# One signal and one read per head for the maxima scores of an attention kernel

## The reference

```python
q = (layer_norm(x) @ q_w); k, v = ctx @ k_w, ctx @ v_w          # 16 heads of 16
s = jnp.einsum('bnhd,bmhd->bhnm', q, k) * scale
s = jnp.where(mask, -big, s)                                    # stages 0, 2, 3
x = x + (jax.nn.softmax(s) @ v) @ proj_w + proj_b
x = x + gelu(layer_norm(x) @ fc1_w + fc1_b) @ fc2_w + fc2_b     # stages 0, 2, 4
```

## Time and profile before

| what | value |
|---|---|
| median of 3 runs | 5233.54 us |
| the profiled execution, by its own time | 5238.51 us |
| its span, first to last instruction | 5236.7 us |
| mean granted TensorE clock | 0.959 of full speed |
| TensorE matmuls busy | 4648.7 us (89%) |
| VectorE busy | 3017.8 us (58%) |
| ScalarE busy | 2310.5 us (44%) |
| stages 0 to 4, about | the first 3960 us |

### The profile page before, as it was taken

The page is one execution under the profiler, slowest core; times in us unless marked ns, Lnnn a source line. Parts: engine busy times, 40 slices in busy tenths (PEclk is TensorE's granted clock), DMA queues, the critical chain, the costliest instruction groups (busy, mean ns, idle before and its releaser), DMA issues.

```text
span 5236.7 us, 70053 instructions
## 1 busy us (share of the span) xinstructions
PE 4648.7 (89%) x24484; PEld 1877.5 (36%) x24484; DVE 3017.8 (58%) x6690; ACT 2310.5 (44%) x3011; POOL 963.7 (18%) x831
## 2 busy tenths in 40 slices
PE   5898898888887989999888888888877999999999
PEld 2333333333332333343444433333333333333333
DVE  5766676556667767666455665445422545554554
ACT  3444454456664444434444444443432433333332
POOL 0111111101110111111111111110111433333333
PEclk9999999999999999999999999999988999999999
DMA  1111111121111100001111211110111000000000
GB/s 55 35 42 56 38 48 42 35 73 65 56 65 48 37 35 31 30 29 51 62 59 57 68 56 45 39 35 33 43 36 52 1 13 13 13 13 13 1 13 9
DMA packets 152323, 201.92 MB, mean 39 GB/s; under 512 B 18993, under 2 KB 102321, under 8 KB 150706
## 3 DMA queue, kind: packets, MB, share of 16 engines
q1 hardware_dynamic: 151986, 197.31, 11.2%
HBM read 128.86 MB, written 68.42 MB: 38 GB/s over the span
## 4 chain that ended last, share of the span: by engine, by line
PE 64%; DVE 14%; issue 12%; ACT 4%; DMA 4%; POOL 1%; SPq 1%; DVEq 0%; ACTq 0%; POOLq 0%
PE psO L707 7%; PE small L635 7%; PE psT L764 6%; PE small L642 6%; PE psS L663 6%; PE psT L682 5%; PE psT L908 4%; DVE out L1141 3%; PE psT L773 3%; PE small L773 3%; DVE nmb L1144 3%; PE psT L635 2%; PE psT L873 2%; PE psO L923 2%; PE psT L642 2%
## 5 line engine op out<-in xcount | busy, mean ns | idle before, releaser
L966 ACT ACTIVATE probs<-psT 128x1024 f32<-128x1024 f32 (+3 forms) x1280 | 1160.9, 961 | 1054.1 <-PE psT L682 858.4
L1144 DVE TENSOR_REDUCE nmb<-psS 128x2 bf16<-128x1024 f32 x512 | 627.8, 1226 | 332.7 <-PE psS L663 331.9
L682 PE MATMUL psT<-low 32*128 32x512 f32 (+3 forms) x5120 | 771.7, 621 | 49.7 <-ACT probs L966 28.2
L1141 DVE CUSTOM_DVE_ANT_0 out<-psS,pens_sb 128x512 f32<-128x512 f32 x1024 | 665.4, 687 | 81.4 <-issue 60.0
L663 PE MATMUL psS<-out 32*128 32x512 bf16 (+3 forms) x2560 | 494.1, 383 | 219.1 <-DVE nmb L1141 121.4
L707 PE MATMUL psO<-probs,V 128*32 128x512 f32 (+3 forms) x5120 | 673.6, 600 | 1.2 <-ACT probs L966 1.0
L1343 DVE TENSOR_REDUCE parts<-psS 128x2 bf16<-128x1024 f32 x256 | 314.9, 1230 | 522.0 <-PE psS L895 522.0
L1081 ACT ACTIVATE probs<-psT 128x1024 f32<-128x1024 f32 x256 | 262.2, 1024 | 526.0 <-PE psT L911 526.0
L663 PEld LDWEIGHTS psS<-out 32*128 32x128 bf16 x2560 | 121.1, 91 | 900.7 <-DVE nmb L1141 367.5
L764 PE MATMUL psT<-out,W 128*128 128x512 f32 x768 | 378.8, 618 | 0.5
L1460 POOL TENSOR_TENSOR oN<-oN,probs 128x1024 f32<-128x1024 f32 x128 | 300.7, 2349 | 316.1 <-ACT probs L1081 315.8
(11 more groups left out here) (163 smaller groups left out, 5822.6 us busy)
## 6 DMA issues: line engine op xcount, KB each, us to landing
o_mid<-out SPq DMA_DIRECT2D x160, 256.0 KB, 2.0
oN<-o_mid SPq DMA_DIRECT2D x160, 128.0 KB
oN<-r_mid SPq DMA_DIRECT2D x80, 256.0 KB
x_mid<-xe SPq DMA_DIRECT2D x40, 512.0 KB, 3.0
xw<-x_mid SPq DMA_DIRECT2D x36, 512.0 KB, 4.0
xe<-x_mid SPq DMA_DIRECT2D x36, 512.0 KB, 4.8
cT<-ctxT SPq DMA_DIRECT2D x20, 512.0 KB, 7.3
W<-wm SPq DMA_DIRECT2D x6, 1024.0 KB, 8.0
```

What stands on the lines that cost most here:

```text
L682: last = nc.tensor.matmul(psT[j][:, q0:S], Kf[rows_of(j), q, a, c, kt * P:(kt + 1) * P], Qf[rows_of(j), q, a, c, q0:S], start=True, stop=p ...
L966: nc.scalar.activation(probs[:, i % 2, two, q0:S], psT_all[:, two, q0:S], ACT.Exp, scale=float(DH) ** -0.5)\
L1141: nc.vector.tensor_tensor_reduce(junk[:, e, 0:n], psS[e][:, 0:n], penalty, 1.0, -3.0e38, ALU.add, ALU.max, nmb4[:, g, qt, at:at + 1]).then ...
L1144: nc.vector.tensor_reduce(nmb4[:, g, qt, row:row + 33:32], psS_both[:, :, 0:n], AX, ALU.max)\
```

## The change

Each head of a pair gets a semaphore of its own in both directions: s_full0 and s_full1, s_read0 and s_read1. TensorE waits for head e's bank in front of head e's matmul, and each matmul signals. VectorE waits for head e's scores in front of head e's read, and each read signals. In stages 1 and 4 the one reduction over 1024 columns becomes two over 512. In stages 0, 2 and 3 each of the two reads gets its own memset and its own wait for the head's read one pair earlier. Fill "m" waits for both semaphores. The function `reads`, which told the two forms' counts apart, goes.

```diff
@@ -254,11 +254,6 @@
 N_WO = C * D + 2 * D
 
 
-def reads(s):
-
-    return 2 if s in (*MASKED, CAUSAL) else 1
-
-
 def per_unit(s):
 
     mlp = 1 if s in MLP else 0
@@ -269,7 +264,7 @@
         "stats": norms, "moments": norms, "variance": norms, "rstd": norms, "normed": norms,
         "stats_m": mlp, "moments_m": mlp, "variance_m": mlp, "rstd_m": mlp, "normed_m": mlp,
         "biased": 1 + mlp, "q_low": C,
-        "s_full": 2 * STEPS, "s_read": 2 * STEPS * reads(s),
+        "s_full0": 2 * STEPS, "s_full1": 2 * STEPS, "s_read0": 2 * STEPS, "s_read1": 2 * STEPS,
         "f_full": FC * mlp, "f_read": FC * mlp, "z_full": mlp, "z_read": mlp,
         "st_full": 2 * STEPS, "exp_done": 2 * STEPS,
         "pv_done": STEPS, "o_out": G, "o_stored0": 32, "o_stored1": 32,
@@ -656,13 +651,12 @@
                         pe.wait_ge(small_read, place.start() + 1)
                     pe.wait_ge(sem["q_low"], count("q_low", u, c + 1))
 
-                if positive(r := count("s_read", u, (2 * i + k) * reads(u.s))):
-                    pe.wait_ge(sem["s_read"], r)
                 for e in range(2):
                     j = 2 * (1 - k) + e
-                    last = nc.tensor.matmul(psS[e][:, 0:n], Qb[rows_of(j), q, a, c, qt * P:(qt + 1) * P], Kb[rows_of(j), q, c, 0:n],
-                                            start=True, stop=True)
-                last.then_inc(sem["s_full"], 1)
+                    if positive(r := count(f"s_read{e}", u, 2 * i + k)):
+                        pe.wait_ge(sem[f"s_read{e}"], r)
+                    nc.tensor.matmul(psS[e][:, 0:n], Qb[rows_of(j), q, a, c, qt * P:(qt + 1) * P], Kb[rows_of(j), q, c, 0:n],
+                                     start=True, stop=True).then_inc(sem[f"s_full{e}"], 1)
 
             def exp_scores(place, u, i):
 
@@ -723,7 +717,8 @@
                 if kind == "k" and use == place.first(who, "k0") and u.s not in OWN_KEYS and u.s:
                     pe.wait_ge(sem["ctx_in"], count("ctx_in", u, 16))
                 if kind == "m":
-                    pe.wait_ge(sem["s_read"], count("s_read", u, 2 * T * (int(use[1]) + 1) * reads(u.s)))
+                    for e in range(2):
+                        pe.wait_ge(sem[f"s_read{e}"], count(f"s_read{e}", u, 2 * T * (int(use[1]) + 1)))
                 if kind == "q" and use == place.first(who, "q0"):
                     pe.wait_ge(qkv_in, 16 * (u.s + 1))
                 if kind == "y" and use == place.first(who, "y"):
@@ -1127,22 +1122,21 @@
                 g, qt = divmod(i, T)
                 n = (qt + 1) * P if u.s == CAUSAL else S
                 row = MAX_ROW[g % 2] + DL * (1 - k)
-                dve.wait_ge(sem["s_full"], count("s_full", u, 2 * i + k + 1))
-                if reads(u.s) == 2:
-                    penalty = tri_row[:, S - n:S] if u.s == CAUSAL else masking(pensM, u)[:, qt * S:(qt + 1) * S]
-                    if u.s == 0 and i == 0 and k == 0:
-                        dve.wait_ge(sem["pens"], count("pens", u, 1))
-
-                    if positive(r := count("s_read", u, 2 * (2 * i + k))):
-                        dve.wait_ge(sem["s_read"], r)
-                    nc.vector.memset(scratch[:, 6:7], 0.0)
-                    for e in range(2):
-                        at = row + 32 * e
+                if u.s == 0 and i == 0 and k == 0:
+                    dve.wait_ge(sem["pens"], count("pens", u, 1))
+                for e in range(2):
+                    at = nmb4[:, g, qt, row + 32 * e:row + 32 * e + 1]
+                    dve.wait_ge(sem[f"s_full{e}"], count(f"s_full{e}", u, 2 * i + k + 1))
+                    if u.s in (*MASKED, CAUSAL):
+                        penalty = tri_row[:, S - n:S] if u.s == CAUSAL else masking(pensM, u)[:, qt * S:(qt + 1) * S]
+
+                        if positive(r := count(f"s_read{e}", u, 2 * i + k)):
+                            dve.wait_ge(sem[f"s_read{e}"], r)
+                        nc.vector.memset(scratch[:, 6 + e:7 + e], 0.0)
                         nc.vector.tensor_tensor_reduce(junk[:, e, 0:n], psS[e][:, 0:n], penalty, 1.0, -3.0e38,
-                                                       ALU.add, ALU.max, nmb4[:, g, qt, at:at + 1]).then_inc(sem["s_read"], 1)
-                else:
-                    nc.vector.tensor_reduce(nmb4[:, g, qt, row:row + 33:32], psS_both[:, :, 0:n], AX, ALU.max)\
-                        .then_inc(sem["s_read"], 1)
+                                                       ALU.add, ALU.max, at).then_inc(sem[f"s_read{e}"], 1)
+                    else:
+                        nc.vector.tensor_reduce(at, psS[e][:, 0:n], AX, ALU.max).then_inc(sem[f"s_read{e}"], 1)
 
             def limit(u, i):
 
```

## The result

The changed kernel takes 5188.3 us (median of 4 runs, 5179.8 to 5195.9) where the kernel before takes 5234.3 beside it: a ratio of 0.991, 95% interval 0.9897 to 0.9923, or 46 us less. The forecast was 5222 and its range began at 5200: the sign was right, the size was not. The profiled execution has a span of 5177.0 us against 5236.7.

What follows compares the result with a forecast made beforehand. TensorE's instruction stream was taken as the bound, with 194 us of idle time before maxima scores all the change could reach. Terms -28 + 7.4 + 3.7 + 5 = -12 us gave 5222 us, range 5200 to 5252.

Steps and rivals of the forecast that it cites:

- first wait: Maxima pair held up for VectorE's read when the pair before was not itself held up; 229 of 324 waited pairs.
- (2): Stages 1 and 4: one reduction becoming two costs 0.07 us at each of 106 first waits, 7.4 us on.
- (3): Stages 0, 2 and 3: one memset more costs 0.03 us at each of 123 first waits, 3.7 us on.
- (4): VectorE already late, with layer-norm work at a unit's start: added work delays what follows, about 5 us on.
- (1): Head 0's matmul starts once its bank is read: no gain at a first wait, 28 us off at 54 second waits.
- second wait: Maxima pair held up for VectorE's read directly behind another held-up pair; 95 of 324 waited pairs.
- (5): Extra waits on TensorE and VectorE and their register operations in loops: costed at nothing, hidden by instructions queued ahead.
- (6): MLP block: TensorE's array has no gap there, so its 16 pairs per unit neither gain nor lose.
- A: Rival, slower: VectorE's second instruction is not overlapped and pays its fixed part at first waits; 5253 us, chance 0.20.
- B: Rival: vanished second waits turn up one step further on; gains halve to 14 against 14 of cost; 5234 us, chance 0.17.
- D: Rival: the wait between a pair's two matmuls pulls them apart in loops, 48 us; 5280 us, chance 0.05.
- C: Rival: added work costs nothing and fewer slow-clock stretches give 5 to 10 us more; 5195 us, chance 0.13.

Runs made afterwards that it cites:

- both_clean: Changed kernel, but TensorE waits once per pair, for head 1's read, in front of both matmuls; 5228.9 us, ratio 0.9988.
- swap_before: Kernel before, but in stages 0, 2 and 3 VectorE waits for its own last reads ahead of the scores, not behind; 5224.3 us, ratio 0.9980.
- both_before: Changed kernel, but TensorE waits for both banks, with two waits, before a pair's first matmul; 5250.7 us, ratio 1.0027.
- after_again: The changed kernel run once more, no edit; 5178.7 us, ratio 0.9900 to the kernel before.
- triple_both: Changed kernel, but at the second and third pair behind each MLP block TensorE waits for both banks; 5211.6 us, ratio 0.9956.
- dve_both: Changed kernel, but VectorE begins a pair only when both heads' scores are there; 5274.3 us, ratio 1.0077.
- plan_before: Kernel before, with only the order of maxima pairs behind the MLP blocks of looped units changed, one pair moved ahead; 5220.6 us, ratio 0.9971.

## Why the prediction was right or wrong, point by point

**The view: right. The bound: wrong.** The maxima waits are where the change acts, and a first wait is the chain that was read. But the 194 us of idle time were not "all that this change can reach": the 430 us at the lower clock were in reach too.

**(2) The split reduction: right.** A first wait in stage 1 in the kernel after:

```profile
1397.65 0.39 PE L658 MATMUL psS<-out 32*128 32x512 bf16 x2
...
1398.10 2.48 DVE L1139 TENSOR_REDUCE nmb<-psS 128x1 bf16<-128x512 f32 x4
...
1398.84 0.39 PE L658 MATMUL psS<-out 32*128 32x512 bf16 x1
...
1399.44 0.38 PE L658 MATMUL psS<-out 32*128 32x512 bf16 x1 [0.21 <-DVE nmb L1139]
```

1.79 us from pair to second matmul (1.79 forecast), and four reductions in 2.48 us: 0.60 apart, 0.68 long. Over the first waits of stages 1 and 4 the delay rose by 5.8 us, 6.5 in both_clean (7.4 forecast). The 125 ns that the Trainium skill gives for VectorE's fixed access cost on PSUM ("Perfetto Trace Analysis", "Optimizing Scalar/DVE Operations") would have made it 13, an estimate from that page; rows and runs say 0.06 to 0.07 us a pair.

**(3) The memset: sign wrong, small.** The masked reductions follow each other 0.62 us apart with the memset between them (601.74, 602.36, ...), against 0.61 before: 0.01 and not 0.03. And first waits in stages 0, 2 and 3 became 8.5 us shorter in all (5.5 in stages 0 and 2, 3.0 in stage 3) where 3.7 more was forecast. In both_clean it is 5.1 shorter. The likeliest reason is the register operation that no longer stands behind the wait for the scores; swap_before shows that it matters pair by pair, and that such a cost is not read from a median.

**(4) VectorE's own sequences: too small.** Pairs that were not late before carry 10.6 us of delay now (8.1 in both_clean); 5 were forecast.

**(1) The early matmul: right in kind, its term 28 us.** Measured 21.4 (both_clean to after). Counting any pair behind a held one as a second wait (113 here, 95 in the prediction), these fell by 20.5 us.

The sum of the delay: 5.8 - 8.5 - 20.5 + 10.6 = -12.6, measured -12.7 pair by pair, forecast -12. The second count has 5.3 - 6.7 - 24.8 + 7.5 = -18.7. So the total is right within 7 us, and that it fits to the microsecond is luck: the errors of (1), (3) and (4) cancel.

**(5) and (6): right for the change.** Pairs in the MLP block are still 2.23 us apart (554.77, 557.00), unhindered matmuls of a pair 0.003 us. What (5) did not see is that the second wait is free because each stands in front of a matmul of its own; both_before shows the price where two stand in front of one, 0.09 us.

**The clock: the step that failed.** The prediction says "What the sum leaves out is TensorE's clock" and allows "+-15 us, in the range, not in the sum". It had the mechanism before it in rows 7, and its bound of 15 on the number of stretches just held: 68 at the low level became 53 (47 in after_again, 21 fewer). Wrong were the price, 0.4 to 1 us a stretch, and that it was given no sign. The low stretch behind rows 7 lasts 3.4 us; the mean of all is 6.3 (430 us in 68). The low time fell by 101 us (136 in after_again). What that is worth: over the 14 profiled executions the span fits a constant + 0.72 x delay + 0.45 x low, residuals up to 10 us (0.73 and 0.44 with the second count, residuals up to 7); with a delay counted in full it is 0.38 for low. A mean stretch then costs 2.4 to 2.8 us, over twice the highest price taken. The 101 us are worth 38 to 45 us, and with the delay's term 51 to 55 of the 60 us between the profiled spans.

The profiled execution of the kernel before is one of its slower ones, and the granted clock is on record for every run, to 0.001. From it the mean low time is 415 us over 67 runs of the kernel before and 327 over 8 of the changed one, 88 less, with spans 53 us apart (5234.4 and 5181.4). And within one kernel, where the program is the same, the span moves by 0.31 us with each us of low time (158 runs of 13 kernels). At 0.31 to 0.45 the 88 us are worth 27 to 40 of the 53, which leaves 13 to 26 for the delay, counted at 12.7 to 18.7.

The Trainium skill, "TensorE: Matmul & The Clock Gate", section "Terms", puts the penalty at the slow time times (1 - K/N), which at half the clock is 0.5; the runs lie below that, at 0.31 to 0.45. That it is because TensorE waits anyway for a part of that time is likely and not shown. This term should have been in the sum, with its sign: second waits stretched out the idle time ahead of a dense stretch (rows 6 and 7, and triple_both), and the change shortens just those.

**The rivals.** A (slower by the second instruction's fixed part) fell with the spacing of 0.60. B (nothing moves) fell. D (the matmuls pulled apart) fell with the 2.23 us pace. C (more) was nearest, and too small even so: it gave the clock 5 to 10 us, took the added work as free, which it isn't (8.7 us), and had a chance of 0.13. Two slips of working changed nothing of this: B's cost is 16.1 us by the terms above it and not 14, so 5236, and its chances by class add up to 0.36, 0.38 and 0.26 rather than 0.40, 0.34 and 0.26.

**The claims.** The triple's third pair 1.3 to 1.4 us behind the second: 1.23. 1280 more instructions, the 0.69 and 0.61 us (0.68 and 0.60): met. First waits grew by 0.06 to 0.07, under the 0.12 that was to be wrong. "TensorE's idle before L663 down from 194 to about 180": 83.7, since that view counts head 0's matmul in the wait as busy; the quantity meant, the delay, fell by 12.7. One of the signs of error that it named came: the slow-clock stretches moved by more than ten.

**What stays open.** Which pattern of gaps decides the level at a place: dve_both fills gaps with a matmul and keeps the low time; the low time of one kernel differs by 35 us between two executions with the same delay. The clock's share is therefore shown as a sum (triple_both, plan_before, the runs within one kernel), not place by place.

## What to carry to other kernels

Where a change shortens gaps ahead of dense TensorE work, compare the time at the lower clock before and after, and put a term for it in the sum: here 0.3 to 0.45 us for each us that leaves the low level, in all about twice the waits themselves or more. Give a second wait its own instruction to stand in front of; two waits before one instruction cost about 0.1 us on the path here. Check what a control kernel adds by itself before its number is believed, even when it is the number expected.

## What the runs showed of the hardware that was not expected

- Two waits in front of one matmul: it starts 0.146 us behind the read instead of 0.057. In front of one reduction: 0.530 us behind the pair instead of 0.427.
- Few gaps move much of the clock: 48 pairs of 1280 changed the low time by 43 to 78 us.
- A us at the lower clock costs less than half a us here: 0.31 us between runs of one kernel, 0.45 between kernels.
- Scatter differs between kernels: 27 us over four runs of after_again, 14 over thirteen of the kernel before beside them. Less waiting is not the reason, as both_clean, with more, has 27 us over twelve.
